# Two narrow self-attentions on one core: scores on 32-row tiles, the mask as a bf16 product, key blocks on GpSimd, Newton steps for the roots

## The chip, the core and the metric

The kernel runs on one core of a Trainium2 chip. The metric is the device time of the whole program in microseconds. A profiled execution gives the span from the first to the last instruction and everything that happened in it.

## The reference, cut to what matters

The program is a decoder layer stack of six phases on 128 sequences of 64 tokens with 128 features: a wide self-attention, a narrow cross-attention, a feed-forward block, two narrow self-attentions (one global, one local), a wide cross-attention and a last product with tanh. Only the two narrow self-attentions change.

```
def rmsnorm(x, w): return x * rsqrt(mean(x * x) + 1e-6) * w
def qk_norm(x):    return x * rsqrt(mean(x * x) + 1e-6)
q = split_heads(x @ wq, 16)          # 16 heads of 8 features
k, v = split_heads(..., 4)           # 4 key/value heads, each for 4 query heads
q, k = qk_norm(rope(q)), qk_norm(rope(k))
scores = where(mask, q @ k.T / sqrt(8), -1e30)   # causal; local: also i - j < 32
out = merge_heads(softmax(scores) @ v) @ wo
...
h = layernorm(x)
h = h + global_attention(rmsnorm(h)); h = h + local_attention(rmsnorm(h)); x = x + h
```

## The kernel before

Activations stay in SBUF: X (`w_x`) and the working copy H (`w_h`), both as 64 tiles of 128 tokens (two sequences) by 128 features. Each phase is a block in which every engine runs its own program, and `narrow_self_attention(k, local)` makes the global stage (tiles named `gl_`) and the local one (`lo_`). In each program `skewed(engine, 64, [(lag, piece), ...], unroll)` writes out the order by hand: in step u the engine runs each piece, in the list's order, on tile u minus its lag. `after(engine, semaphore, t, back)` makes the engine wait until tile t-back has passed a point. An engine's queue is in order, so a waiting piece holds back everything behind it in its list.

The path of a tile, with lines of the kernel before:
- VectorE normalises it. In the global stage it takes statistics of X, GpSimd takes the root (`rsqrt`, L1832), VectorE writes H (L1699), then takes the root mean square of H by a second set of statistics (L1707 to L1726), GpSimd takes that root (`rms_rsqrt`, L1838), VectorE writes `hn` (L1732). The local stage has the second half alone.
- TensorE turns `hn` (`turn`, L1571), ScalarE copies it out (L1634), TensorE projects to queries, keys and values (L1579, 192 columns).
- VectorE rotates queries and keys (L1739 to L1749), squares them (L1756) and sums each head (L1762, 20 columns); GpSimd raises the 20 sums to the power -0.5 (`qk_rsqrt`, L1844); VectorE multiplies (`qk_apply`, L1775 and L1776).
- TensorE transposes the queries in four pieces of 32 columns and the keys in one (L1587, L1588). ScalarE copies the queries (L1650, 32x512) and writes the keys four times, scaled by a 0/1 column per key head, so that the other heads' rows are zero (`key_blocks`, L1658).
- `scores` (L1597) is four fp32 products of 128 weight columns by 256 query columns, run as eight passes. Rows 64 to 127 of both operands hold an identity and the mask, written once at the start (L1805 to L1814), so that the same product adds the mask. Each half goes to its own PSUM bank and ScalarE takes the exponential of each (L1666).
- ScalarE spreads the values out (L1642, four short copies), TensorE multiplies probabilities and values (`attend`, L1609, 32 passes), VectorE divides (L1782, L1789), TensorE turns it (L1617), ScalarE copies (L1672), TensorE applies the output weights (L1622), and VectorE adds the residual (L1795 or L1797).

Other phases have instructions of the same kinds: the narrow cross-attention scores on 32-row tiles and makes its key blocks on GpSimd (L1245), the wide one scores on 64-row tiles (L845) and scales its probabilities on GpSimd (L1016). Every normalisation there adds epsilon and takes a root on GpSimd (L486, L489), and VectorE applies it (L496).

## Time and profile before

| what | us |
|---|---|
| median of 3 runs (2473.71 to 2476.63) | 2474.64 |
| the profiled execution, its own time | 2471.66 |
| its span | 2469.6 |
| TensorE busy over the span | 2181.6 (88%) |
| VectorE busy | 1927.5 (78%) |
| ScalarE busy | 1490.9 (60%) |
| GpSimd busy | 1224.1 (50%) |

In the rows, PE is TensorE's products and PEld its weight loads, DVE is VectorE, ACT is ScalarE, POOL is GpSimd. "128*64" is the part of the array in use, "<-" reads "written from". Idle time before a group is followed by what ended most of it. The global stage lies at about 1081 to 1400 us of the span, the local one at 1401 to 1705.

### The profile page before, as it was taken

To read this page: it belongs to the slowest core of one execution; us is meant where nothing else is said; L and a number is where in the kernel's file an instruction comes from. 1 tells how busy PE (TensorE), PEld (TensorE's weight loads), DVE (VectorE), ACT (ScalarE), POOL (GpSimd) and SP (SyncE) were. 2 spreads that over 40 slices of the span, in tenths; PEclk is the share of its full clock that TensorE was granted. 3 is DMA by queue.
4 is the path that set the end of the run, shared out by engine and by line. 5 is a ranking of instruction groups with operands and counts; after the bars stand their busy time and mean duration, and the time that the engine had idled before them with its cause. 6 is when DMAs were issued, how large, how long until landed. Compare 5 with 4: busy or idle time off the path is not lost. (4 is left out here: it accounts for less than half of the span.)

```text
span 2469.6 us, 90130 instructions
## 1 busy us (share of the span) xinstructions
PE 2181.6 (88%) x33103; PEld 1800.1 (73%) x33103; DVE 1927.5 (78%) x5481; ACT 1490.9 (60%) x3973; POOL 1224.1 (50%) x1215
## 2 busy tenths in 40 slices
PE   7999999977777753439999799998999999999998
PEld 7888888865555541228888588886888888888886
...
DMA packets 56943, 25.66 MB, mean 10 GB/s; under 512 B 18115, under 2 KB 56326, under 8 KB 56838
## 3 DMA queue, kind: packets, MB, share of 16 engines
...
q14 instruction: 38, 0.31, 0.0%
...
## 5 line engine op out<-in xcount | busy, mean ns | idle before, releaser
L706 POOL TENSOR_TENSOR sa_sc<-sa_sc,sa_rs 128x1024 f32<-128x1024 f32 x64 | 121.9, 1904 | 314.3 <-DVE sa_rs L682 314.3
L1844 POOL TENSOR_TENSOR lo_qk_r<-lo_qk_ms,w_neg_half 128x20 f32<-128x20 f32 x64 | 226.8, 3544 | 21.9 <-DVE lo_qk_ms L1767 21.9
L1844 POOL TENSOR_TENSOR gl_qk_r<-gl_qk_ms,w_neg_half 128x20 f32<-128x20 f32 x64 | 227.0, 3546 | 1.4 <-DVE gl_qk_ms L1767 1.3
L486 POOL TENSOR_TENSOR xan_ve<-xan_mv,w_eps_ln 128x1 f32<-128x1 f32 x64 | 12.1, 189 | 400.5 <-DVE xan_mv L480 400.5
L892 ACT ACTIVATE xa_cT<-xa_misc 128x128 f32<-128x128 f32 x64 | 17.8, 277 | 304.9 <-PE xa_misc L793 273.6
L1016 POOL TENSOR_TENSOR xa_sc<-xa_sc,xa_rs 128x1024 f32<-128x1024 f32 x64 | 121.7, 1902 | 119.1 <-DVE xa_rs L976 119.1
L821 PEld LDWEIGHTS xa_qs<-xan_xT,late_x_wq 128*128 128x128 f32 x1024 | 120.0, 193 | 52.8 <-issue 52.8
L973 DVE TENSOR_REDUCE xa_sm<-xa_sc 128x16 f32<-128x1024 f32 x64 | 78.1, 1220 | 71.6 <-ACT xa_sc L916 71.6
L1236 POOL TENSOR_TENSOR ca_sc<-ca_sc,ca_mx 128x1024 f32<-128x1024 f32 x64 | 121.8, 1902 | 24.1 <-DVE ca_mx L1206 24.1
L558 PE MATMUL sa_qs<-san_xT,w_a_wq 128*128 128x128 f32 x1024 | 130.3, 281 | 2.7 <-DVE sa_sc L668 2.2
L821 PE MATMUL xa_qs<-xan_xT,late_x_wq 128*128 128x128 f32 x1024 | 132.2, 283 | 0.0
L832 PE MATMUL xa_pp<-xa_cT,late_x_wk 128*128 128x128 f32 x1024 | 131.1, 281 | 0.0
L1597 PE MATMUL lo_ss<-lo_qT,lo_kz 128*128 128x256 f32 x512 | 127.9, 393 | 1.3 <-ACT lo_kz L1658 0.9
L878 PE MATMUL xa_yy<-late_x_wo,xa_oT 128*128 128x128 f32 x1024 | 126.6, 277 | 2.5 <-ACT xa_oT L930 2.5
L1597 PE MATMUL gl_ss<-gl_qT,gl_kz 128*128 128x256 f32 x512 | 127.4, 392 | 1.3 <-ACT gl_kz L1658 0.9
L930 ACT ACTIVATE xa_oT<-xa_oo 128x512 f32<-128x512 f32 x128 | 69.4, 594 | 97.6 <-PE xa_oo L868 97.6
L810 PE MATMUL xa_oo<-late_x_wv,xa_cT 128*64 128x512 f32 x512 | 125.7, 612 | 0.7 <-ACT xa_cT L892 0.7
L603 PE MATMUL sa_yy<-w_a_wo,sa_oT 128*128 128x128 f32 x1024 | 124.9, 275 | 1.2 <-ACT sa_oT L651 1.2
L679 DVE TENSOR_REDUCE sa_sm<-sa_sc 128x16 f32<-128x1024 f32 x64 | 78.1, 1220 | 59.2 <-ACT sa_sc L637 59.2
L558 PEld LDWEIGHTS sa_qs<-san_xT,w_a_wq 128*128 128x128 f32 x1024 | 120.7, 194 | 4.8 <-DVE sa_sc L668 4.8
L878 PEld LDWEIGHTS xa_yy<-late_x_wo,xa_oT 128*128 128x128 f32 x1024 | 121.1, 194 | 2.7 <-ACT xa_oT L930 2.7
L832 PEld LDWEIGHTS xa_pp<-xa_cT,late_x_wk 128*128 128x128 f32 x1024 | 119.1, 191 | 4.2
...
## 6 DMA issues: line engine op xcount, KB each, us to landing
...
```

Source lines behind the costliest of these rows:

```text
L558: last = pe.matmul(qs[b][:, c * P:(c + 1) * P], k["a_wq"][:, ch * P:(ch + 1) * P], norm["xT"][:, s, :], start=True, stop=True)
L603: last = pe.matmul(yy[:, 0:D], oT[:, s, n % 2, n // 2, :], k["a_wo"][:, n, :], start=(n == 0), stop=(n == 7))
L679: dve.tensor_reduce(sm[:, s, :], sc[:, s, :, :, :].rearrange("p e c j -> p (e c) j"), AX.X, ALU.add).then_inc(sum_done, 1)
L706: pool.tensor_tensor(v, v, bcast(rs[:, s, :], 2, S), ALU.mult).then_inc(prob_done, 1)
L810: final = pe.matmul(oo[order][r * 64:r * 64 + 64, :].rearrange("p (m c) -> p m c", m=4), cT[:, s, b * 64:b * 64 + 64], wv[:, :, r, :], sta ...
L821: final = pe.matmul(qs[b][:, c * P:(c + 1) * P], k["x_wq"][:, ch * P:(ch + 1) * P], norm["xT"][:, s, :], start=True, stop=True)
L832: final = pe.matmul(pp[b][:, c * P:(c + 1) * P], k["x_wk"][:, ch * P:(ch + 1) * P], cT[:, s, :], start=True, stop=True)
L878: final = pe.matmul(yy[:, 0:D], oT[:, s, n % 2, n // 2, :], k["x_wo"][:, n, :], start=(n == 0), stop=(n == 7))
L1016: pool.tensor_tensor(v, v, bcast(rs[:, s, :], 2, S), ALU.mult).then_inc(prob_done, 1)
L1236: pool.tensor_tensor(sc[:, four, :, :], sc[:, four, :, :], bcast(mx[:, s, :], 2, S), ALU.subtract).then_inc(shifted, 1)
L1597: last = pe.matmul(ss[b][:, g * 256:(g + 1) * 256], kz[:, s, b, 2 * g:2 * g + 2, :].rearrange("p g j -> p (g j)"), qT[:, s, b, :, :].rearr ...
L1844: pool.tensor_tensor(qk_r[:, s, :], qk_ms[:, s, :], k["neg_half"][:, 0:NQK], ALU.pow).then_inc(sg["qk_r"], 1)
```

## The change

- The mask is no longer part of the scores' operands. Four bf16 products of an identity with the mask (`identb`, `maskb`) start the four PSUM banks, one for each query head of a group; 16 fp32 products on 32-row tiles, one tile for each such head, add the scores. One semaphore step reports all of them.
- Queries and keys are transposed by two products of 128 columns; the keys are written four times side by side by VectorE (`kn`). ScalarE copies both in one instruction. GpSimd writes the key blocks in one multiplication of 128x512.
- The 20 roots for each tile are no longer a power. VectorE halves the sums and makes a first guess by integer arithmetic on their bits, for two tiles at once; GpSimd refines it by three Newton steps of four instructions on 40 columns, each waiting for the one before.
- In the global stage the second set of statistics goes: both roots come from the first variance, in one power of two columns, and `hn` is written from X.
- One PSUM bank (`tr`) holds the first transpose and the two of queries and keys, with waits that keep their writes and reads apart. Lags and orders change; TensorE and ScalarE are unrolled by eight, with eight value buffers.

```diff
+SEED = float(0x5f3759df - 0x400000)
...
+        identb, maskb = sb("identb", [P, P], BF16), sb("maskb", [P, 4, S], BF16)
...
-                    pe.transpose(misc[:, 0:P], hn[:, s, :], ident).then_inc(sg["hT_psum"], 1)
+                    after(pe, sg["qT"], t, 6)
+                    pe.transpose(tr[:, 0:P], hn[:, s, :], ident).then_inc(sg["hT_psum"], 1)
...
                     after(pe, sg["qkn"], t, per=2)
                     after(pe, sg["qT"], t, 1)
-                    after(pe, sg["k_blocks"], t, 1, per=KVG)
+                    pe.wait_ge(sg["hT"], min(t + 5, NT) if isinstance(t, int) else t + 5)
+                    pe.transpose(tr[:, P:2 * P], qn[:, s, :, :, :].rearrange("p r g d -> p (r g d)"), ident)
+                    pe.transpose(tr[:, 2 * P:3 * P], kn[:, s, :, :, :].rearrange("p r g d -> p (r g d)"), ident).then_inc(sg["qkT_psum"], 1)
+                def scores(t, four):
+                    s = four % 2
+                    after(pe, sg["exp"], t, 1, per=2)
                     for r in range(4):
-                        pe.transpose(tq[0:32, r * P:(r + 1) * P], qn[:, s, r, :, :].rearrange("p g d -> p (g d)"), ident)
-                    pe.transpose(tk[0:32, 0:P], kn[:, s, :, :].rearrange("p g d -> p (g d)"), ident).then_inc(sg["qkT_psum"], 1)
-                def scores(t, four):
-                    s = four % 2
+                        pe.matmul(ss[:, r, 0:256], identb[:, :], maskb[:, :, :].rearrange("p n i -> p (n i)"), start=True, stop=False)
                     after(pe, sg["qT"], t)
-                    after(pe, sg["k_blocks"], t, per=KVG)
+                    after(pe, sg["k_blocks"], t)
+                    gate(k, pe)
                     for b in range(2):
-                        after(pe, sg["exp"], t, 1, per=2)
                         for g in range(2):
-                            last = pe.matmul(ss[b][:, g * 256:(g + 1) * 256],
-                                             kz[:, s, b, 2 * g:2 * g + 2, :].rearrange("p g j -> p (g j)"),
-                                             qT[:, s, b, :, :].rearrange("p r i -> p (r i)"), start=True, stop=True)
-                        last.then_inc(sg["scores_psum"], 1)
...
+                                                 kz[q, s, b, 2 * g:2 * g + 2, :].rearrange("p g j -> p (g j)"),
+                                                 qkT[q, s, 0, b * 64:b * 64 + 64], start=False, stop=(b == 1 and g == 1))
+                    last.then_inc(sg["scores_psum"], 1)
...
-                skewed(pe, NT, [(4, turn_queries_keys), (6, turn_out), (2, project), (5, attend), (6, output), (1, turn), (4, scores)], 4)
+                skewed(pe, NT, [(6, turn_queries_keys), (1, turn), (2, project), (7, attend), (8, turn_out), (6, scores), (8, output)], 8)
...
-                def queriesT(t, four):
+                def queries_keysT(t, four):
...
-                    after(act, sg["scores_psum"], t, 2, per=2)
-                    act.activation(qT[0:32, s, :, :, :].rearrange("p b r i -> p r b i"),
-                                   tq[0:32, :].rearrange("p (r b i) -> p r b i", r=4, b=2), ACT.Copy).then_inc(sg["qT"], 1)
...
-                    after(act, sg["scores_psum"], t, 2, per=2)
-                    for g in range(KVG):
-                        act.activation(kz[0:32, s, :, g, :], tk[0:32, 0:P].rearrange("p (b j) -> p b j", b=2), ACT.Copy,
-                                       scale=groups[0:32, g:g + 1]).then_inc(sg["k_blocks"], 1)
+                    act.wait_ge(sg["hT_psum"], min(t + 6, NT) if isinstance(t, int) else t + 6)
+                    after(act, sg["scores_psum"], t, 2)
+                    after(act, sg["k_blocks"], t, 2)
+                    act.activation(qkT[:, s, :, :].rearrange("p n i -> p (n i)"), tr[:, P:3 * P], ACT.Copy).then_inc(sg["qT"], 1)
...
-                    for b in range(2):
-                        act.wait_ge(sg["scores_psum"], t * 2 + b + 1)
-                        act.activation(pr[:, s, :, b, :], ss[b][:, :].rearrange("p (n i) -> p n i", i=S), ACT.Exp,
+                    after(act, sg["scores_psum"], t)
+                    for r in (0, 2):
+                        act.activation(pr[:, s, r:r + 2, :, :, :].rearrange("p r b g i -> p r (b g i)"), ss[:, r:r + 2, 0:256], ACT.Exp,
...
-                skewed(act, NT, [(4, queriesT), (6, outT), (4, key_blocks), (2, values), (1, turned), (4, exponent)], 4)
+                skewed(act, NT, [(6, queries_keysT), (1, turned), (8, outT), (2, values), (6, exponent)], 8)
...
+                    dve.tensor_scalar(ve[:, s, 0:1], mv[:, s, 1:2], EPS_LN, None, ALU.add).then_inc(sg["var_eps"], 1)
+                    dve.tensor_scalar(ve[:, s, 1:2], mv[:, s, 1:2], 1.0 + EPS_RMS, EPS_LN * EPS_RMS, ALU.mult,
...
-                    dve.tensor_scalar(tile_of(H, t), tile_of(X, t), mv[:, s, 0:1], rstd[:, s:s + 1],
+                    after(dve, sg["hT_psum"], t, 2)
+                    dve.tensor_scalar(hn[:, s, :], tile_of(X, t), mv[:, s, 0:1], rstd[:, s, 1:2],
+                                      ALU.subtract, ALU.mult).then_inc(sg["normed"], 1)
...
+                def hidden_itself(t, four):
+                    s = four % 2
+                    dve.tensor_scalar(tile_of(H, t), tile_of(X, t), mv[:, s, 0:1], rstd[:, s, 0:1],
                                       ALU.subtract, ALU.mult).then_inc(sg["hidden"], 1)
...
-                    after(dve, sg["squared"], t, 2)
...
+                    after(dve, sg["qkn"], t, 4, per=2)
+                    dve.tensor_tensor(rot[:, four, :, :], rc[:, s, :, :], rsn[:, s, :, :], ALU.add).then_inc(sg["rotated"], 1)
...
-                def qk_epsilon(t, four):
...
-                    dve.tensor_scalar(qk_ms[:, s, :], qk_ms[:, s, :], HD * EPS_RMS, None, ALU.add).then_inc(sg["qk_mse"], 1)
+                    dve.tensor_reduce(qk_ms[:, four, :], sq[:, s, :, :], AX.X, ALU.add).then_inc(sg["qk_ms"], 1)
...
+                def qk_halve(t, four):
+                    if four % 2:
...
+                        dve.tensor_scalar(qk_half[:, p, :], qk_ms[:, p, :], HD * EPS_RMS, 0.5, ALU.add, ALU.mult).then_inc(sg["qk_half"], 2)
+                def qk_seed(t, four):
...
+                        dve.tensor_scalar(qk_r[:, p, :].bitcast(I32), qk_half[:, p, :].bitcast(I32), -0.5, SEED, ALU.mult,
+                                          ALU.add).then_inc(sg["qk_seed"], 2)
...
-                    dve.tensor_tensor(kn[:, s, :, :], rot[:, s, HEADS:NQK, :], bcast(qk_r[:, s, HEADS:NQK], 2, HD), ALU.mult).then_inc(sg["qkn"], 1)
+                    dve.tensor_tensor(kn[:, s, :, :, :], bcast(rot[:, four, HEADS:NQK, :], 1, 4),
+                                      bcast(bcast(qk_r[:, four, HEADS:NQK], 2, HD), 1, 4), ALU.mult).then_inc(sg["qkn"], 1)
...
-                dve.memset(qT[:, :, :, :, :], 0.0).then_inc(sg["zeroed"], 1)
-                dve.memset(kz[:, :, :, :, :], 0.0).then_inc(sg["zeroed"], 1)
-                dve.wait_ge(sg["zeroed"], 3)
-                for n in range(2):
-                    for b in range(2):
-                        dve.tensor_copy(qT[64:P, n, b, :, :], bcast(ident[64:P, 64:P], 1, 4)).then_inc(sg["masked"], 1)
-                        dve.tensor_copy(kz[64:P, n, b, :, :], bcast(mask[64:P, :], 1, KVG)).then_inc(sg["masked"], 1)
+                dve.tensor_copy(identb[:, :], ident).then_inc(sg["masked"], 1)
+                dve.tensor_copy(maskb[:, :, :], bcast(mask, 1, 4)).then_inc(sg["masked"], 1)
...
-                    skewed(dve, NT, [(4, qk_apply), (7, residual), (0, rms_measure), (1, rms_apply), (7, residual_x), (0, rms_mean),
+                    skewed(dve, NT, [(6, qk_apply), (1, rms_apply), (9, residual), (0, rms_measure), (9, residual_x), (0, rms_mean),
                                      (2, rotate), (0, rms_square), (2, rotate_sum), (0, rms_epsilon), (2, qk_measure),
-                                     (5, invert_sums), (2, qk_sum), (5, divide), (2, qk_epsilon)], 4)
+                                     (7, invert_sums), (2, qk_sum), (7, divide), (2, qk_halve), (2, qk_seed)], 4)
                 else:
-                    skewed(dve, NT, [(6, qk_apply), (9, residual), (0, hidden), (1, normed_hidden), (3, rms_apply), (0, hidden_mean),
-                                     (2, rms_measure), (0, hidden_epsilon), (2, rms_mean), (4, rotate), (2, rms_square),
-                                     (4, rotate_sum), (2, rms_epsilon), (4, qk_measure), (7, invert_sums), (4, qk_sum),
-                                     (7, divide), (4, qk_epsilon)], 4)
+                    skewed(dve, NT, [(6, qk_apply), (1, normed_hidden), (9, residual), (0, hidden), (1, hidden_itself),
+                                     (0, hidden_mean), (2, rotate), (0, hidden_epsilon), (2, rotate_sum), (2, qk_measure),
+                                     (7, invert_sums), (2, qk_sum), (7, divide), (2, qk_halve), (2, qk_seed)], 4)
...
+                    after(pool, sg["rms_var_eps"], t)
                     after(pool, sg["hidden"], t, 2)
-                    pool.tensor_tensor(rstd[:, s:s + 1], ve[:, s:s + 1], k["neg_half"][:, 0:1], ALU.pow).then_inc(sg["rstd"], 1)
+                    after(pool, sg["normed"], t, 2)
+                    pool.tensor_tensor(rstd[:, s, :], ve[:, s, :], k["neg_half"][:, 0:2], ALU.pow).then_inc(sg["rstd"], 1)
...
-                    pool.tensor_tensor(qk_r[:, s, :], qk_ms[:, s, :], k["neg_half"][:, 0:NQK], ALU.pow).then_inc(sg["qk_r"], 1)
-                shift = 0 if local else 2
-                front = [] if local else [(0, rsqrt)]
-                skewed(pool, NT, front + [(shift, rms_rsqrt), (2 + shift, qk_rsqrt)], 4)
+                    if four % 2 == 0:
+                        return
+                    p = slice(four - 1, four + 1)
+                    y, y2 = qk_r[:, p, :], qk_a[:, p, :]
+                    for n in range(3):
+                        if n == 0:
+                            after(pool, sg["qk_seed"], t)
+                        else:
+                            pool.wait_ge(sg["qk_step"], t - 1 + n)
+                        done = (t - 1) * 3 + 2 * n + 2
+                        pool.tensor_tensor(y2, y, y, ALU.mult).then_inc(sg["qk_y2"], 2)
+                        pool.wait_ge(sg["qk_y2"], done)
+                        pool.tensor_tensor(y2, y2, qk_half[:, p, :], ALU.mult).then_inc(sg["qk_hy2"], 2)
+                        pool.wait_ge(sg["qk_hy2"], done)
+                        pool.tensor_tensor(y2, three_halves[:, :, :], y2, ALU.subtract).then_inc(sg["qk_rest"], 2)
+                        pool.wait_ge(sg["qk_rest"], done)
+                        last = pool.tensor_tensor(y, y, y2, ALU.mult)
+                        if n < 2:
+                            last.then_inc(sg["qk_step"], 1)
+                        else:
+                            last.then_inc(sg["qk_r"], 2)
+                def key_blocks(t, four):
+                    s = four % 2
+                    after(pool, sg["qT"], t)
+                    after(pool, sg["scores_psum"], t, 2)
+                    pool.tensor_tensor(kz[:, s, :, :, :].rearrange("p b g j -> p g b j"),
+                                       bcast(qkT[:, s, 1, :].rearrange("p (b j) -> p b j", b=2), 1, KVG),
+                                       bcast(bcast(groups, 2, 2), 3, S), ALU.mult).then_inc(sg["k_blocks"], 1)
+                pool.memset(three_halves[:, :, :], 1.5).then_inc(sg["constant"], 1)
+                pool.wait_ge(sg["constant"], 1)
+                skewed(pool, NT, [(6, key_blocks), (0, rms_rsqrt if local else rsqrt), (2, qk_rsqrt)], 4)
```

## Rows read from the trace of the kernel before

**Rows 1.** Busy us by window: PE, PEld, DVE, ACT, POOL, then granted clock; global, local
```profile
...
1200.00:1360.00 160.00, 158.80 (x1793) 129.36 (x1791) 134.37 (x739) 133.97 (x458) 160.00 (x107) 1.00 0.00 0
...
1500.00:1650.00 150.00, 150.00 (x1738) 126.24 (x1737) 108.37 (x615) 128.60 (x445) 138.16 (x70) 1.00 0.00 0
...
```

**Rows 2.** Timeline of GpSimd, global stage, one tile: start us, length us, instruction
```profile
...
1247.26 3.53 POOL L1844 TENSOR_TENSOR gl_qk_r<-gl_qk_ms,w_neg_half 128x20 f32<-128x20 f32 x1
1250.77 0.54 POOL L1832 TENSOR_TENSOR gl_rstd<-gl_ve,w_neg_half 128x1 f32<-128x1 f32 x1
1251.28 0.62 POOL L1838 TENSOR_TENSOR gl_rms<-gl_ms,w_neg_half 128x1 f32<-128x1 f32 x1
1251.80 3.53 POOL L1844 TENSOR_TENSOR gl_qk_r<-gl_qk_ms,w_neg_half 128x20 f32<-128x20 f32 x1
...
```

**Rows 3.** Timeline of TensorE, local stage, one tile: start, length, instruction, count
```profile
...
1553.04 1.96 PE L1597 MATMUL lo_ss<-lo_qT,lo_kz 128*128 128x256 f32 x8
1554.84 0.60 PE L1587 MATMUL lo_tq<-w_constant,lo_qn 128*32 128x128 f32 x4
...
1555.39 0.27 PE L1617 MATMUL lo_yy<-w_constant,lo_o 128*128 128x128 f32 x1
1555.50 0.49 PE L1579 MATMUL lo_qkv<-w_s_w,lo_hT 128*128 128x192 f32 x2
1555.92 1.11 PE L1609 MATMUL lo_av<-lo_vz,lo_pr 128*64 128x18 f32 x32
1556.96 0.49 PE L1622 MATMUL lo_yy<-w_s_wo,lo_oT 128*128 128x128 f32 x2
1557.29 0.27 PE L1571 MATMUL lo_misc<-w_constant,lo_hn 128*128 128x128 f32 x1
1557.43 1.97 PE L1597 MATMUL lo_ss<-lo_qT,lo_kz 128*128 128x256 f32 x8
```

**Rows 4.** Groups of ScalarE, local stage, 1500 to 1650: busy us, mean ns | idle
```profile
...
L1666 ACT ACTIVATE lo_pr<-lo_ss 128x512 f32<-128x512 f32 x68 | 40.6, 597 | 17.8 <-PE lo_ss L1597 17.8
...
L1642 ACT ACTIVATE lo_vz<-lo_qkv 64x16 f32<-64x16 f32 x138 | 24.0, 174 | 2.5
...
```

**Rows 5.** Line L1597, scores: min/median/max ns, first and last start in us
```profile
...
L1597 PE MATMUL gl_ss<-gl_qT,gl_kz x512: 379/379/767, 1107.8 to 1395.7; 128*128 128x256 f32 x171
...
L1597 PE MATMUL lo_ss<-lo_qT,lo_kz x512: 379/379/767, 1418.9 to 1699.9; 128*128 128x256 f32 x171
...
```

**Rows 6.** Timeline of VectorE at the start of the local stage
```profile
...
1401.24 0.30 DVE L1805 MEMSET lo_vz<- 128x288 f32 x1 [0.94 <-PEq L164]
...
1405.77 0.29 DVE L1707 BATCH_NORM_STATS2 lo_rstats<-w_h 128x6 f32<-128x128 f32 x1
```

**Rows 7.** Timeline of TensorE, wide cross-attention: scores on 64-row tiles, next instruction
```profile
...
2004.30 1.16 PE L845 MATMUL xa_qs<-xa_kT,xa_qT 64*64 64x64 f32 x64
2005.44 0.30 PE L779 MATMUL xa_misc<-w_constant,xan_xn 128*128 128x128 f32 x1
...
```

**Rows 8.** Line L1154, ScalarE's copy of 128x256 from PSUM
```profile
...
L1154 ACT ACTIVATE ca_xcT<-ca_m x64: 382/383/402, 549.2 to 885.1; 128x256 f32<-128x256 f32 x64
...
```

**Rows 9.** Line L1245, GpSimd's key blocks of the narrow cross-attention
```profile
...
L1245 POOL TENSOR_TENSOR ca_kz<-ca_kT,w_constant x64: 1041/1042/1045, 551.8 to 890.1; 128x512 f32<-128x512 f32 x64
...
```

**Rows 10.** Timeline of GpSimd, wide cross-attention: one instruction, one that needs it
```profile
...
1904.93 0.19 POOL L486 TENSOR_TENSOR xan_ve<-xan_mv,w_eps_ln 128x1 f32<-128x1 f32 x1 [6.13 <-DVE xan_mv L480]
1905.20 0.55 POOL L489 TENSOR_TENSOR xan_rstd<-xan_ve,w_neg_half 128x1 f32<-128x1 f32 x1
...
```

**Rows 11.** Line L1016, GpSimd's product of 128x1024
```profile
...
L1016 POOL TENSOR_TENSOR xa_sc<-xa_sc,xa_rs x64: 1899/1902/1905, 1725.0 to 2448.8; 128x1024 f32<-128x1024 f32 x64
...
```

**Rows 12.** Timeline of GpSimd, narrow cross-attention: the same two instructions
```profile
...
730.44 0.19 POOL L486 TENSOR_TENSOR can_ve<-can_mv,w_eps_ln 128x1 f32<-128x1 f32 x1 [0.99 <-DVE can_mv L480]
730.78 0.55 POOL L489 TENSOR_TENSOR can_rstd<-can_ve,w_neg_half 128x1 f32<-128x1 f32 x1 [0.16 <-POOL can_ve L486]
...
```

**Rows 13.** Line L496, VectorE's normalisation in the wide cross-attention
```profile
...
L496 DVE TENSOR_SCALAR xan_xn<-w_x,xan_mv,xan_rstd x64: 340/997/1009, 1707.3 to 2428.2; 128x128 f32 x48, 128x128 f32<-128x128 f32 x16
...
```

85 lines of the change are left out of this document (43 added, 42 removed).

## The prediction

> **What bounds the kernel now.** I read the busy time by window first. The two self-attention stages are steady, at the full 2.4 GHz clock. In the global stage GpSimd is busy for all of 160 us and TensorE for 158.8; in the local stage TensorE for all of 150 us, GpSimd for 138 and ScalarE for 129 [rows 1]. So there are two near-equal bounds, and the reader has to look inside a tile to see which sets the period. In the global stage GpSimd runs one 3.53 us power on 20 columns and two of about 0.54 us on one column, back to back, and starts the next tile's 4.54 us after the last [rows 2]: GpSimd is the bound. In the local stage TensorE has no gap in a tile of 4.39 us [rows 3]: scores 1.80 (1553.04 to 1554.84), five transposes of queries and keys 0.55, transpose of the output 0.11, projection 0.42, values product 1.04, output 0.33, first transpose 0.14. ScalarE's exponentials take 0.597 us each, two a tile [rows 4]. From first to last score, 63 intervals, the stages take 287.9 and 281.0 us [rows 5]. The profiled execution took 2471.66 us around a span of 2469.6; the median of the runs is 2474.64, 3.0 more. I work the sum on the profiled one and add 3.0.
>
> **The change, part by part.** *TensorE's own work.* Three of five transposes go (3 x 0.11); two remain, of 128 columns, taken as 0.12 each: 0.24 for 0.55 [rows 3]. The eight score passes of 256 columns, 0.225 each [rows 3], give way to four bf16 mask products of 256 columns and 16 products on 32-row tiles, which as fp32 are 32 passes. No row has a bf16 product here: at most one fp32 pass each (0.90 for four), at least a quarter of the time of both passes of a product (0.45). I take 0.45, since these need one pass of 256 columns where the fp32 form needs two slower ones. For the 32 passes the nearest row is the wide cross-attention's 64 passes on four 64x64 tiles, 1.14 us with the change-over at both ends, 0.94 without [rows 7]: 0.059 a pass on its own tile. There too a tile has 64 moving columns, but 64 weight columns; here it has 128. If the weights set the pace a pass takes twice as long: eight to a tile, 8 x 0.118 = 0.94; if the moving columns do, 0.47. I take 0.94, and 0.1 for each change of tile shape (half of 1.14 less 0.94). TensorE's sum falls from 4.39 to 4.39 - 0.31 - 1.80 + 0.45 + 0.94 + 0.20 = 3.87.
>
> The Trainium skill, "TensorE: Matmul & The Clock Gate", section LDWEIGHTS, says a load's time follows its columns, not its rows, so cutting products to 32 rows would save nothing on loads. By that, with the tiles loading in turn, the 32 passes would cost 32 x 0.107 = 3.4 us, an estimate from that page. The 64 passes in [rows 7] fit tiles that load beside each other; that case is priced as a rival.
>
> *ScalarE.* The four scaled copies of the keys go and the 512-column copy becomes one of 256 columns, 0.38 [rows 8]. The values' four short copies and the exponentials stay [rows 4]. Its sum falls well under the period; only the order of its work matters below.
>
> *GpSimd.* Key blocks: 128x512 with two broadcasts, the same instruction shape as the narrow cross-attention's, 1.04 us a tile [rows 9]. Newton: 12 dependent products of 40 columns for each pair of tiles, each waiting for the one before by a semaphore. A one-column instruction lasts 0.19 and the next, dependent one starts 0.27 after it [rows 10]; per column the long form costs (1.902 - 1.042) / 512 = 1.7 ns [rows 9, 11], so 40 columns add 0.06: 0.33 each, 12 x 0.33 = 3.96 a pair. Below, 0.27 if the columns are free (3.24); above, 0.34 [rows 12] plus 0.06 plus rounding, 0.41 (4.92). The global stage's power on two columns costs 0.54 + 0.16 (a column is (3.53 - 0.54) / 19) = 0.70, the local one's 0.54 [rows 2]. A pair of global tiles is 2 x (1.04 + 0.70) + 3.96 = 7.44, or 3.7 a tile where it was 4.54. By sums alone everything gets faster.
>
> *VectorE.* The global stage loses the second set of statistics, the local one nothing much; the additions in small columns go to pairs, the keys' product grows from 32 to 128 columns (about 0.1). It was busy 134 of 160 us [rows 1] and falls; its cover is the period itself, and I cost it at nothing as long as a tile lasts over 4 us. The two memsets of 0.91 and eight copies ahead of the stage give way to two copies: 4.5 us of setup [rows 6] becomes about 1.7, a gain of 2.8. No DMA is added or moved.
>
> **The order of the work is what I think decides.** Keys now pass through four engines, and GpSimd's queue is in order: key blocks of tile u-6, the root of tile u, and on odd steps the whole Newton chain. Two loops follow, with handoffs of 0.05 to 0.1.
> Loop A, key blocks to the next key blocks: blocks 1.04, to TensorE 0.10, scores' products to their last result 0.94 + 0.22, to ScalarE 0.05, two exponentials 1.15, then, behind them in ScalarE's queue, the next queries-and-keys copy 0.33, to GpSimd 0.08: 3.91.
> Loop B, scores to scores: 1.16 + 0.05 + 1.15, to TensorE 0.07, values product 1.04 (it stands ahead of the scores in TensorE's queue and waits for the exponentials), output transpose 0.11, masks 0.45, change-over 0.10: 4.13. So TensorE's 3.87 is not reached; 4.13 would be.
> On an odd step GpSimd does blocks 1.04, root 0.70, chain 3.96 and 0.08 of handoff, 5.78, before it can take the next blocks, although these are ready after 3.9. TensorE waits for them with the scores, and behind them stand output, the next transposes, projection and values: nothing can run ahead, so the late time isn't made up on the even step, when GpSimd idles. A pair takes 5.78 + 3.91 = 9.69 us in the global stage and 9.53 in the local one (root 0.54), 4.84 and 4.77 a tile against 4.54 and 4.39. Key blocks of tile t run in step t+6 and chains in the odd steps 3 to 65, so the intervals after tiles 1, 3 ... 59 carry a chain, 30 of the 63: global 30 x 9.69 + 3 x 4.13 = 303.1, +15.2; local 30 x 9.53 + 12.4 = 298.3, +17.3 [rows 5]. Front edge: locally scores begin two steps later; four steps took 1405.77 to 1418.9, 3.3 each [rows 5, 6], so 6.6 less 2.8 of setup, +3.8; globally the depth stays at six and I put +1 for the chains. Sum +37.3: 2509.0 for the profiled execution, 2512 as a median. The new waits of the shared transpose bank (queries-and-keys copy behind the next first transpose) ask only for a 0.11 us transpose that directly follows; nothing.
>
> **Rivals.**
> 1. *Forecast, the chain blocks the key blocks* (chance 0.52): 2512, from 2469 (3.24 a chain: 60 chains x 0.72 = 43 less) to 2570 (4.92: 58 more).
> 2. *The burst is absorbed* (0.27), the other side: the place is GpSimd's queue between two key blocks. If the chain is short enough, or the loop through ScalarE long enough, that 5.78 fits, a pair takes 2 x 4.13 = 8.26. Global 63 x 4.13 = 260.2, -27.7; local -20.8; with edges +4.8, -43.7: 2431. For it: all sums fall, and one-off spans on GpSimd are rough. Against: [rows 10] have even a one-column instruction at 0.27. It decides from where a pair falls 37.3 / 60 = 0.62 under my 9.6, to about 9.0: a chain of some 3.3 us.
> 3. *The chain waits for VectorE* (0.12). A normalisation from SBUF to SBUF took 0.997 us beside GpSimd's long product and 0.340 otherwise [rows 13]: the two engines do hold each other up. If each chain product meets such a VectorE instruction 40% of the time (some six a tile, near 0.3 us like the one in [rows 6], in 4.8) and waits half of it, that is 0.06 x 12 = 0.7 a pair, +43: 2555. Against: the 3.53 us powers keep their length with VectorE's additions beside them [rows 2].
> The Trainium skill, "SBUF — State Buffer", section "Who interferes with whom", has this rule: VectorE instructions with two SBUF inputs, or in a two-port mode, lock GpSimd out. The trace bears out the second half only, and only in the other direction.
> 4. *Row tiles load in turn* (0.04): 32 passes of 0.118 are 3.8 us, 2.8 more. In a pair the chain hides this on one tile; on the other it lengthens loop A: 60 x 2.8 = 168, about 2680. [Rows 7] speak against it.
> 5. *It nets out* (0.05): shorter handoffs and a chain near 3.3.
>
> **Numbers.** Predicted 2512. The range 2440 to 2572 holds the forecast's own 2469 to 2570, rival 3 and the upper part of rival 2. Measurements tell 0.2%, 5 us, from no change. Faster 0.29 (rival 2, a little of 1), within 0.07, slower 0.64.
>
> **What the next profile would show.** Right: GpSimd's chain of 12 in a row, then key blocks at once; TensorE's scores waiting for key blocks on every second tile for 1.5 us or so, tile spacings alternating near 4 and 5.7; TensorE's busy share in both stages at some 80%. Wrong: even spacings near 4.1; chain products starting under 0.28 apart; scores' products far from 1 us; the values product waiting where I have the scores wait.

## The result: 2809 us where 2475 stood and 2512 was forecast

The changed kernel takes 2809.0 us in the median (2808.1 to 2809.3, three runs) against 2474.64: a ratio of 1.1355, 95% interval [1.1338, 1.1373]. The sign was forecast, the size was not: the result lies 237 us above the top of the range. The profiled execution has a span of 2807.2 us, 337.6 more than before.

The page of the changed kernel's profile, engine totals and three lines of the 40 slices:

```profile
PE 2503.7 (89%) x36303; PEld 2068.2 (74%) x36303; DVE 1991.5 (71%) x5273; ACT 1329.2 (47%) x3461; POOL 1099.3 (39%) x1921
...
PE   7999999877777243999999699999989999999998
...
POOL 0333333377776301444444344444312222222222
PEclk8999999999999675555555555555589999999999
```

Read the last line first. Over both narrow stages, slices 16 to 29 of the 40, the granted clock of TensorE is 5 tenths, 1.2 GHz, where it was 9 or more before outside the stage borders. TensorE's digits beside it are 9, but for the stage borders. Both kernels enter the global stage at 0.5; this is the kernel before, just ahead of its first scores (busy time of PE, PEld, DVE, ACT, POOL, then the clock):

```profile
1094.00:1108.00 14.00, 5.54 (x16) 3.15 (x17) 11.59 (x64) 4.17 (x19) 10.63 (x10) 0.50 0.00 0
```

It came to 1.0 at about 1114 us and kept it to the stage's end. The changed kernel never came to it. One stretch in each of its stages, the answer to [rows 1]:

```profile
1250.00:1400.00 150.00, 150.00 (x1627) 124.56 (x1627) 89.08 (x389) 54.09 (x193) 73.38 (x175) 0.50 0.00 0
1700.00:1850.00 150.00, 150.00 (x1633) 124.37 (x1630) 87.66 (x385) 53.71 (x194) 70.97 (x175) 0.50 0.00 0
```

TensorE is busy in every microsecond, GpSimd for half of them. The line of the scores' products, the answer to [rows 5], says what this costs:

```profile
L1606 PE MATMUL gl_ss<-gl_qkT,gl_kz x2048: 416/416/472, 1122.6 to 1561.8; 32*128 32x64 f32 x187
...
L1606 PE MATMUL lo_ss<-lo_qkT,lo_kz x2048: 416/416/472, 1597.5 to 2036.6; 32*128 32x64 f32 x187
```

First to last score: 439.2 and 439.1 us where there were 287.9 and 281.0, that is +151.3 and +158.1. The first score comes 14.8 later, the gap between the stages is 12.5 longer, and behind the last score 0.9 is added: together 337.6, the whole difference. The per-tile work is in the timeline of TensorE, one global tile, the answer to [rows 3]:

```profile
1300.52 1.90 PE L1618 MATMUL gl_av<-gl_vz,gl_pr 128*64 128x18 f32 x32
1302.35 0.48 PE L1626 MATMUL gl_yy<-w_constant,gl_o 128*128 128x128 f32 x1
1302.62 1.06 PE L1598 MATMUL gl_ss<-gl_maskb,gl_identb 128*128 128x256 bf16 x4
1303.61 1.99 PE L1606 MATMUL gl_ss<-gl_qkT,gl_kz 32*128 32x64 f32 x32
1305.53 0.80 PE L1631 MATMUL gl_yy<-w_s_wo,gl_oT 128*128 128x128 f32 x2
1306.12 0.42 PE L1591 MATMUL gl_tr<-w_constant,gl_qn 128*128 128x128 f32 x1
1306.33 0.42 PE L1592 MATMUL gl_tr<-w_constant,gl_kn 128*128 128x128 f32 x1
1306.54 0.42 PE L1576 MATMUL gl_tr<-w_constant,gl_hn 128*128 128x128 f32 x1
1306.76 0.85 PE L1584 MATMUL gl_qkv<-w_s_w,gl_hT 128*128 128x192 f32 x2
1307.53 1.90 PE L1618 MATMUL gl_av<-gl_vz,gl_pr 128*64 128x18 f32 x32
```

Take start to start: values 1.83, masks 0.99, scores 1.92, and so on to 7.0 us a tile (1300.52 to 1307.53), with no gap. The forecast's sum has 1.04, 0.45 and 1.04 for these three, at 2.4 GHz: each takes about twice as long. GpSimd's timeline (the chain's first products, then the key blocks behind its last one) has the structure of the forecast in it all the same:

```profile
1310.62 0.25 POOL L1862 TENSOR_TENSOR gl_qk_a<-gl_qk_r 128x40 f32<-128x40 f32 x1 [1.17 <-DVE gl_qk_r L1779]
1311.02 0.27 POOL L1864 TENSOR_TENSOR gl_qk_a<-gl_qk_a,gl_qk_half 128x40 f32<-128x40 f32 x1
1311.43 0.27 POOL L1866 TENSOR_TENSOR gl_qk_a<-gl_three_halves,gl_qk_a 128x40 f32<-128x40 f32 x1
...
1314.97 0.27 POOL L1868 TENSOR_TENSOR gl_qk_r<-gl_qk_r,gl_qk_a 128x40 f32<-128x40 f32 x1
1315.20 1.04 POOL L1878 TENSOR_TENSOR gl_kz<-gl_qkT,w_constant 128x512 f32<-128x512 f32 x1
```

The products last 0.25 to 0.27 but start 0.35 to 0.41 apart: a chain is 4.6 us from 1310.62 to the key blocks at 1315.20. At 1.2 GHz TensorE's 14 us a pair hide it.

### The profile page after: what moved, and what is told of

The parts are those of the page before. It is cut to its first block and busy times, and to the rows that moved or that the text cites. A ratio compares the mean times of both kernels' runs of the same rounds, so it can differ in the third digit from the quotient of the medians.

```text
span 2807.2 us, 96939 instructions
## 1 busy us (share of the span) xinstructions
PE 2503.7 (89%) x36303; PEld 2068.2 (74%) x36303; DVE 1991.5 (71%) x5273; ACT 1329.2 (47%) x3461; POOL 1099.3 (39%) x1921
## 5 line engine op out<-in xcount | busy, mean ns | idle before, releaser
L1606 PEld LDWEIGHTS lo_ss<-lo_qkT,lo_kz 32*128 32x128 f32 x2048 | 115.2, 323 | 29.4 <-issue 29.4
L1606 PEld LDWEIGHTS gl_ss<-gl_qkT,gl_kz 32*128 32x128 f32 x2048 | 115.1, 323 | 29.4 <-issue 29.4
L1618 PEld LDWEIGHTS lo_av<-lo_vz,lo_pr 128*64 128x64 f32 x2048 | 114.5, 224 | 28.7 <-issue 25.0
L1618 PEld LDWEIGHTS gl_av<-gl_vz,gl_pr 128*64 128x64 f32 x2048 | 114.5, 224 | 28.7 <-issue 25.0
L1237 POOL TENSOR_TENSOR ca_sc<-ca_sc,ca_mx 128x1024 f32<-128x1024 f32 x64 | 121.8, 1903 | 23.9 <-DVE ca_mx L1207 23.8
L1667 ACT ACTIVATE lo_pr<-lo_ss 128x512 f32<-128x512 f32 x128 | 69.5, 595 | 129.0 <-PE lo_ss L1606 129.0
L1606 PE MATMUL lo_ss<-lo_qkT,lo_kz 32*128 32x64 f32 x2048 | 127.2, 423 | 3.2 <-issue 3.2
L1606 PE MATMUL gl_ss<-gl_qkT,gl_kz 32*128 32x64 f32 x2048 | 127.2, 423 | 3.2 <-issue 3.2
L1667 ACT ACTIVATE gl_pr<-gl_ss 128x512 f32<-128x512 f32 x128 | 69.5, 595 | 127.4 <-PE gl_ss L1606 127.4
L1878 POOL TENSOR_TENSOR gl_kz<-gl_qkT,w_constant 128x512 f32<-128x512 f32 x64 | 68.4, 1069 | 147.2 <-ACT gl_qkT L1660 145.1
```

What stands on the lines that cost most here:

```text
L1237: pool.tensor_tensor(sc[:, four, :, :], sc[:, four, :, :], bcast(mx[:, s, :], 2, S), ALU.subtract).then_inc(shifted, 1)
L1606: last = pe.matmul(ss[:, r, (2 * b + g) * 64:(2 * b + g) * 64 + 64], kz[q, s, b, 2 * g:2 * g + 2, :].rearrange("p g j -> p (g j)"), qkT[q, ...
L1618: last = pe.matmul(av[b * 64:b * 64 + 64, n * 2 * VW:(n + 1) * 2 * VW], pr[:, s, n % 4, b, n // 4, :], vz[:, eight, n // 4, b, :, :].rearr ...
L1667: act.activation(pr[:, s, r:r + 2, :, :, :].rearrange("p r b g i -> p r (b g i)"), ss[:, r:r + 2, 0:256], ACT.Exp, scale=HD * float(HD) ** ...
```

## Experiments

Two questions: what keeps the clock down, and what the change is worth where the clock is full. The times are of one execution each, but for the last kernel; the kernel before took 2465 to 2477 us beside them. Where the text gives a time per tile for a whole stage, it is first to last score over the 63 intervals. Some recorded expectations have 5.53, 5.33, 4.54 and 7.26 us instead. These were taken between ScalarE's first and last copies of `hT`, which take in the quick first steps and leave out the last ones; the scores of the same runs give 5.67, 5.55, 4.64 and 7.61. "Parted" stands for a Newton chain parted over two steps.

### Does the level keep itself, or does the stream of products lose it?

The changed kernel with one burst of dense products in each stage:

```diff
+                    if isinstance(t, int) and t == 9:
+                        for n in range(24):
+                            pe.matmul(ss[:, n % 4, 256:512], ident, k["constant"][:, 0:256], start=True, stop=True)
```

> The changed kernel, with 24 dense fp32 products of 256 columns into unused PSUM columns, once in each stage, at step 15 ahead of the masks (extra work, results unused). The changed kernel had a granted clock of 0.50 from 1024 us to 2052 us, all of both stages. Theory C (the stream is too light: the new mix of products never earns the 2.4 GHz level, whatever came before): the clock may rise during the burst and falls back, tile spacing stays near 7.0 us, total 2805 to 2840 us. Theory H (either level keeps itself: the stream would hold 2.4 GHz if it once had it): clock 1.0 behind the burst to the end of the stage, about 50 tiles of each stage at 4.8 to 5.3 us, total 2560 to 2620 us.

Measured: 2825.05 us, inside the range of theory C. By window, before the burst, behind it, and later (columns as above):

```profile
1150.00:1189.00 39.00, 39.00 (x390) 32.34 (x389) 20.21 (x95) 13.29 (x49) 18.27 (x44) 0.50 0.01 2
1190.00:1213.00 23.00, 20.47 (x268) 16.86 (x266) 11.28 (x52) 7.30 (x27) 7.56 (x18) 1.00 0.01 2
1220.00:1400.00 180.00, 180.00 (x1944) 149.39 (x1942) 106.07 (x461) 65.22 (x234) 86.96 (x206) 0.50 0.00 0
```

The clock came, stayed 23.9 us in each stage, and went. Behind the burst stand the products of the changed kernel, and in the first stage the level fell at 1213.9, at the end of TensorE's first long pause behind a chain (the 2.73 us below). These 24 us also show the change itself at 2.4 GHz, TensorE first, then GpSimd:

```profile
1197.57 0.60 PE L1601 MATMUL gl_ss<-gl_maskb,gl_identb 128*128 128x256 bf16 x4
1198.10 1.12 PE L1609 MATMUL gl_ss<-gl_qkT,gl_kz 32*128 32x64 f32 x32
...
1202.40 1.12 PE L1609 MATMUL gl_ss<-gl_qkT,gl_kz 32*128 32x64 f32 x32
...
1213.97 1.98 PE L1609 MATMUL gl_ss<-gl_qkT,gl_kz 32*128 32x64 f32 x32 [2.73 <-issue]
```
```profile
1205.16 1.04 POOL L1881 TENSOR_TENSOR gl_kz<-gl_qkT,w_constant 128x512 f32<-128x512 f32 x1 [2.52 <-ACT gl_qkT L1663]
...
1212.83 1.04 POOL L1881 TENSOR_TENSOR gl_kz<-gl_qkT,w_constant 128x512 f32<-128x512 f32 x1
```

Masks 0.53 for four, scores 4.30 apart without a chain, key blocks 7.67 apart with one; TensorE idles 2.73 us before the scores behind the chain. The scores before that pause start 4.31 apart (1202.40 to 1206.71), those across it 7.26.

Two dense float32 products a tile, whose result nobody reads, ahead of the masks:

```diff
...
+                    for n in range(2):
+                        pe.matmul(ss[:, n, 256:512], ident, k["constant"][:, 0:256], start=True, stop=True)
```

> The changed kernel with two dense fp32 products of 256 columns more in every tile (extra work, results unused). If the clock stays at 0.50 they cost 1.8 us a tile: 128 x 1.8 = 230 more, about 3040 us. Theory C: the added dense work earns the clock back, granted clock 1.0 in both stages, and although there is more work the time falls, to about 2500 to 2570 us (tile 4.6 to 5.3 us, set by GpSimd's chain ahead of the key blocks as I forecast). A theory that TensorE is slow for another reason (row tiles, code fetch) gives 3040.

The changed kernel with identity and mask as float32 (eight dense passes for four):

```diff
-        identb, maskb = sb("identb", [P, P], BF16), sb("maskb", [P, 4, S], BF16)
+        identb, maskb = sb("identb", [P, P]), sb("maskb", [P, 4, S])
```

> The changed kernel with identity and mask in fp32 instead of bf16, one part undone. At half clock the four products take twice 0.99 us: 128 x 0.99 = 127 more, about 2935 us, if the clock stays down. Theory C: eight dense passes instead of four may earn the clock back; then about 2500 to 2570 us. If it was the bf16 type itself that cost the clock, this alone brings it back.

Measured: 2662.45 and 2651.11 us. More work on TensorE, and 147 and 158 us less time; both lie over theory C's 2500 to 2570, by 92 and 81. The window 1200 to 1350, first of the fill, then of the float32 mask:

```profile
1200.00:1350.00 150.00, 129.46 (x2122) 106.51 (x2121) 104.33 (x483) 64.26 (x242) 90.37 (x216) 1.00 0.00 0
```
```profile
1200.00:1350.00 150.00, 139.72 (x2122) 116.04 (x2121) 109.20 (x475) 63.52 (x239) 90.09 (x213) 1.00 0.00 0
```

TensorE is busy for a smaller share than in the changed kernel and has the full clock. (With the fill the level was not quite steady: over the two stages it averaged 0.95 and 0.94, with the float32 mask 1.00 and 0.98.) GpSimd in the float32 mask's run:

```profile
1302.55 1.09 POOL L1878 TENSOR_TENSOR gl_kz<-gl_qkT,w_constant 128x512 f32<-128x512 f32 x1
...
1306.41 1.04 POOL L1878 TENSOR_TENSOR gl_kz<-gl_qkT,w_constant 128x512 f32<-128x512 f32 x1 [2.08 <-ACT gl_qkT L1660]
...
1309.06 0.25 POOL L1862 TENSOR_TENSOR gl_qk_a<-gl_qk_r 128x40 f32<-128x40 f32 x1 [0.87 <-DVE gl_qk_r L1779]
...
1313.84 1.10 POOL L1878 TENSOR_TENSOR gl_kz<-gl_qkT,w_constant 128x512 f32<-128x512 f32 x1
```

Key blocks 3.86 apart without a chain (forecast: 3.91), 7.43 with one (5.78), of which 0.87 is a wait for VectorE's seed and 4.78 the chain. So at full clock too the chain decides, and harder than forecast: 5.67 us a tile in this stage.

### Is it the amount of work or its kind?

Each bfloat16 mask product twice in a row, and, in a kernel of its own, each set of score products twice:

```diff
+                        pe.matmul(ss[:, r, 0:256], identb[:, :], maskb[...], start=True, stop=True)
```
```diff
+                    for twice in range(2):
...
```

> The changed kernel with each of its four bfloat16 mask products issued twice in a row, the second added onto the first, so that the mask counts double in the scores (the output is therefore that of a doubled mask). It asks whether TensorE's clock came back in the run with the mask in float32 because the products are of another type, or because they keep TensorE at work longer. The bfloat16 products took 0.99 us for four at 1.2 GHz. If the amount of work is what matters (theory C in its plain form), the granted clock returns to 2.4 GHz over most of the stages and the time falls to 2620 to 2720 us. If four more bfloat16 products bring nothing, the clock stays at 0.5 and 128 tiles pay 0.9 to 1.0 us each: 2809 + 115 to 127 = 2925 to 2940 us.

(In the edit both products of a bank start it anew, so the second replaces the first and the mask counts once. The work on TensorE is the doubled one all the same.)

> The changed kernel with its 32 score products on 32 rows issued twice over, the second set added onto the first (so the scores count double against the mask and the output is that of doubled scores). Each set took 1.92 us at 1.2 GHz and 1.05 at 2.4. It asks whether more float32 work of the narrow kind brings the clock back, as four wide float32 mask products do. If any float32 work counts alike, the 32 more products (1.05 us at full clock, against 1.4 for the float32 masks) bring 2.4 GHz over most of the stages and the time lies between 2640 and 2760 us. If products that read 32 rows and few columns weigh as little as the first set seems to, the clock stays at 0.5 and 128 tiles pay 1.9 us each: 2809 + 245 = 3040 to 3070 us.

Measured: 2916.96 and 3053.74 us, the second reading of each (the doubled masks 8 us under its lower end). The doubled masks in 1200 to 1350:

```profile
1200.00:1350.00 150.00, 150.00 (x1531) 122.67 (x1532) 73.51 (x343) 47.85 (x171) 63.48 (x150) 0.50 0.00 1
```

Neither brought the clock back at all. The doubled masks are as many passes, of the same rows and columns, as the four float32 products that lift it; the doubled scores are float32, but narrow, and add 1.71 us a tile at 1.2 GHz (8.72 for 7.01 in most steps). So in these runs added busy time alone did not lift the clock; the kind of product matters.

### What the chain costs at full clock

The float32 mask again, six of the chain's twelve products in step t + 2 and six in t + 3 (the semaphores between them stay):

```diff
-                skewed(pool, NT, [(6, key_blocks), (0, rms_rsqrt if local else rsqrt), (2, qk_rsqrt)], 4)
+                skewed(pool, NT, [(6, key_blocks), (0, rms_rsqrt if local else rsqrt),
+                                  (2, lambda t, four: newton(t, four, 0)), (3, lambda t, four: newton(t, four, 1))], 4)
```

> The changed kernel with the mask in float32 (granted clock 1.0 in most of both stages, 2651.1 us) and GpSimd's twelve Newton operations of a pair parted over two steps: six behind the values of step t + 2 and six a step later. It asks whether the chain, standing whole ahead of one tile's key blocks, is what still holds that kernel at 5.53 us a tile. The forecast's own theory: a pair costs one loop of 3.9 and one of 7.2 now, and with six operations (6 x 0.41 = 2.46) in each step, step for step about 1.04 + 2.46 + values behind the wait fit beside the other engines' 4.4 to 4.9; so 4.6 to 5.0 us a tile, in all 2651 - 128 x 0.55 to 0.9 = 2535 to 2580 us. The rival: the order in which the engines pass a tile round, or VectorE, holds the kernel, and the chain only fills GpSimd's idle time; then the time stays within 15 us of 2651.

Measured: 2612.68 us, 38 less, 27.7 of it between the stages' first and last scores (now 5.55 and 5.50 us a tile); that is half the least gain of the first reading, and more than the rival allows. Most of what holds it now is TensorE's own sum with float32 masks, busy for 142.1 of 150 us (1250 to 1400): 1.82 for the masks, start to start, in place of 0.53 adds 1.29 to a tile of about 3.94 (1198.10 to 1202.40 above, less a wait of 0.36), which makes 5.23.

### One or two of the four mask products in float32

Parted chain, with one and with two of the four mask products in float32:

```diff
+                        if r < 1:
+                            pe.matmul(ss[:, r, 0:256], ident, mask32[:, :, :].rearrange("p n i -> p (n i)"), start=True, stop=False)
+                        else:
                             pe.matmul(ss[:, r, 0:256], identb[:, :], maskb[...], start=True, stop=False)
```

> The changed kernel with the Newton chain parted over two steps, as in the run that took 2612.7 us and 5.33 us a tile with all four mask products in float32; here only one of the four is in float32 and three are in bfloat16. A float32 mask product took 0.47 us there (1.89 for four at 2.4 GHz), a bfloat16 one should take about 0.12 at 2.4 GHz (0.25 at 1.2 GHz). If one dense float32 product a tile keeps the 2.4 GHz level, TensorE's sum is 5.33 - 3 x 0.35 = 4.28 us; with GpSimd's 5.8 to 6.3 a pair and the loops between, 4.3 to 4.7 us a tile, in all 2612.7 - 128 x 0.63 to 1.03 = 2480 to 2532 us. If it is too little, the stages run at 1.2 GHz, where TensorE's 7.01 us a tile grow by one product at the half clock: 2800 to 2900 us. Anything between means that the level changes to and fro.

> As the one before, with two of the four mask products in float32 and two in bfloat16. Two float32 products added to the changed kernel brought 2.4 GHz back over most of the stages. Where the level holds: 5.33 - 2 x 0.35 = 4.63 us a tile, 4.6 to 4.9 with the loops, 2525 to 2560 us. If the level changes to and fro, 2600 us or more.

Measured: two, 2542.98 us, inside the first reading, clock 1.0 in both stages but for the global stage's first 16 us. One, 2695.33 us, between its two readings, and this is the strangest profile of the study; one window of each stage:

```profile
1200.00:1350.00 150.00, 145.26 (x2478) 114.62 (x2481) 136.35 (x580) 78.78 (x293) 110.30 (x259) 1.00 0.00 0
1600.00:1750.00 150.00, 150.00 (x1514) 122.05 (x1514) 74.06 (x351) 49.47 (x175) 64.52 (x158) 0.50 0.00 0
```

The same code and the same products: the first stage keeps 2.4 GHz from its first scores to its end (4.64 us a tile), the second 1.2 GHz to its end (7.61). So the kernel ran again with the burst in the second stage alone:

```diff
+                    if local and isinstance(t, int) and t == 9:
+                        for n in range(24):
...
```

> The run with one float32 mask product a tile took 2695.3 us: its first stage ran wholly at the granted clock of 1.0 from 1118 us on, at 4.54 us a tile, its second wholly at 0.5, at 7.26 us a tile, though both issue the same products. Here 24 dense float32 products of 256 columns stand once, at step 15 of the second stage alone (about 9 us), in columns that nobody reads. After such a burst the changed kernel, with no float32 product of that kind, held 2.4 GHz for 23.9 us and fell back. Theory now: with one dense product a tile the stream lies at the edge and the level keeps itself (at 1.0 the same products follow each other faster); then the second stage stays at 1.0 after the burst, some 48 tiles save 2.7 us each, and the time is 2695 + 9 - 130 = 2560 to 2600 us. The rival: the second stage's stream is too light whatever the level before it, and the clock falls back within some 30 us: 2695 to 2710 us.

Measured: 2553.17 us, 7 under the first reading's lower end. The second stage before and after the burst:

```profile
1440.00:1490.00 50.00, 49.91 (x504) 40.05 (x504) 25.51 (x119) 17.09 (x61) 23.26 (x58) 0.50 0.01 2
1510.00:1660.00 150.00, 141.95 (x2323) 113.88 (x2324) 123.26 (x526) 72.09 (x265) 96.12 (x233) 1.00 0.00 1
```

The 24 products that nobody reads took 12.4 us, the first of them at 1.2 GHz, and brought 142 back. The first stage, which has no burst here, rose by itself again. The first burst run's answer ("the level does not keep itself") was right for that stream only: this one holds either level, whichever it is put on.

### Is it the pause behind the chain?

The changed kernel with its bfloat16 masks and the parted chain (the edit of the run that parts the chain, above, alone), and the same with the first burst's edit too:

> The changed kernel with nothing else altered than GpSimd's Newton chain, parted over two steps (all four mask products stay in bfloat16). At 1.2 GHz TensorE's sum of 7.01 us a tile hides the chain in either form, so if the clock stays at 0.5 the time stays at 2795 to 2815 us. If it is the pause behind the whole chain that keeps the clock down, the granted clock comes to 1.0 in both stages, at 4.3 to 4.6 us a tile: 2470 to 2520 us.

> As the run before, with 24 dense float32 products once in each stage at step 15, as in the burst runs. If the pause behind the whole chain is what let the clock fall back after 23.9 us there, it now stays at 1.0 from about 1190 us on in the first stage and in the second: some 48 tiles of each stage at 4.3 to 4.5 us instead of 7, 2809 + 18 - 96 x 2.6 = 2560 to 2600 us. If a stream with no dense float32 mask product is too light whatever its pauses, the clock falls back within some 30 us in each stage: 2800 to 2830 us. A level that holds for some 100 us and then falls would say that it is near the edge.

Measured: 2800.8 us, at 1.2 GHz throughout both stages, inside the first range, and 2666.12 us, between its two. With the burst:

```profile
1200.00:1300.00 100.00, 95.39 (x1641) 73.42 (x1640) 91.48 (x390) 53.83 (x196) 74.97 (x175) 1.00 0.00 1
1320.00:1370.00 50.00, 48.26 (x837) 37.15 (x835) 46.11 (x198) 27.16 (x99) 37.96 (x89) 1.00 0.00 0
...
1700.00:1850.00 150.00, 150.00 (x1619) 124.46 (x1617) 80.96 (x383) 54.54 (x193) 70.23 (x171) 0.50 0.00 0
```

By the trace's record of the granted clock it held 242 us in the first stage, to 1420, some seven us behind the last projection and ahead of the last four tiles' scores, and 68 in the second, against 23.9 twice with the whole chain. This is the third outcome named. The pause behind the whole chain therefore goes with a shorter time at full clock, but without it the stream is still not one that rises to 2.4 GHz by itself, and it may fall from it.

It also gives the price of the changed order at full clock with the worst of the chain gone: 4.60 us a tile (43 tiles, 1203.3 to 1396.3), no better than the 4.54 of before in that stage [rows 2]. TensorE is at 95 of 100 us and VectorE at 91.5, and TensorE's largest wait for another engine there is for VectorE's keys (groups of TensorE, 1200 to 1400; after the bar, idle time and releaser):

```profile
L1591 PE MATMUL gl_tr<-w_constant,gl_qn 128*128 128x128 f32 x44 | 14.4, 328 | 8.4 <-DVE gl_kn L1792 8.2
```

### The other parts alone

The Newton steps put into the kernel before, with that kernel's own order of steps, scores and key blocks (two lines of the edit):

```diff
...
-                                     (7, divide), (4, qk_epsilon)], 4)
+                                     (7, divide), (4, qk_halve), (4, qk_seed)], 4)
```

> The kernel before with the Newton steps on tile pairs alone; scores, key blocks on ScalarE and normalisations as before. Theory C: TensorE's stream is the one of before, so the clock stays at 1.0. GpSimd's 4.54 us a tile in the global stage fall to about 3.6, TensorE's 4.39 is left: 64 x 0.15 = 10 less, local stage within 5 us: 2455 to 2475 us. If the Newton burst is what costs the clock, this run shows 0.5 in both stages and over 2700 us.

Measured: 2986.43 us, a clear miss. Waits of 1150 to 1350 us (waited for: total, times, longest):

```profile
DVE gl_qn L1787 <- POOL gl_qk_r L1869: 53.4, 11, 4.9
...
PE gl_tq L1592 <- DVE gl_kn L1788: 47.7, 11, 4.4
```

In that order VectorE wants the roots of a pair at once after it has made the seed, so every pair stalls all engines for a chain, 4.9 us. TensorE was busy 151 of 200 us and its clock averaged 0.70: the record has 6.8 us at 1.0 and 10.2 at 0.5 in turn, once for each pair. I had taken the chain's length without looking at the steps between seed and use. So next, with the steps that the change has (scores and keys at 6, values product at 7, output at 8) and its fused normalisation (TensorE's line of the edit):

```diff
...
-                skewed(pe, NT, [(4, turn_queries_keys), (6, turn_out), (2, project), (5, attend), (6, output), (1, turn), (4, scores)], 4)
+                skewed(pe, NT, [(6, turn_queries_keys), (8, turn_out), (2, project), (7, attend), (8, output), (1, turn), (6, scores)], 8)
```

> The kernel before with its own scores, masks and key blocks, and from the change only the Newton steps on tile pairs, the fused normalisation in both stages, and the later steps for scores, attention and output that the change gives them. So the products that TensorE runs are those of before. It asks whether the new scores alone took TensorE's clock down, and whether the Newton steps are harmless once a whole step lies between seed and use. Theory C: the granted clock is 1.0 over both stages (after the same dip at a stage's start) and the tiles pass at 4.35 to 4.45 us in both stages: 2455 to 2480 us. If the Newton steps hold the loop all the same, as they did with the old steps (2986 us), the tiles pass at 5 us or more and the time is over 2550 us, whatever the clock.

And the fused normalisation alone, with the old power for queries and keys (its first lines):

```diff
...
-                    dve.tensor_scalar(ve[:, s:s + 1], mv[:, s, 1:2], EPS_LN, None, ALU.add).then_inc(sg["var_eps"], 1)
+                    dve.tensor_scalar(ve[:, s, 0:1], mv[:, s, 1:2], EPS_LN, None, ALU.add).then_inc(sg["var_eps"], 1)
+                    dve.tensor_scalar(ve[:, s, 1:2], mv[:, s, 1:2], 1.0 + EPS_RMS, EPS_LN * EPS_RMS, ALU.mult,
+                                      ALU.add).then_inc(sg["rms_var_eps"], 1)
...
```

> The kernel before with one thing from the change: the first stage takes both of its normalisations from one set of moments, with one root of two columns on GpSimd, and passes its tiles at the local stage's steps. Scores, mask, roots of queries and keys stay. The first stage now passes a tile in 4.54 us and the second, which has that normalisation already in part, in 4.39. If VectorE's shorter chain is what parts the two, 64 tiles gain up to 0.15 us each and the time falls by up to 10 us, to 2464 to 2470 us (ratio 0.996 to 0.998). If TensorE's sum alone sets both, the time stays within 2 us of the kernel before.

Measured: 2481.28 us, and 2463.33 (nine runs), ratio to the 2472.14 of before beside it 0.9965 [0.9954, 0.9976]; the first 1 us over its range, the second 1 under. The scores' lines of the two:

```profile
L1602 PE MATMUL gl_ss<-gl_qT,gl_kz x512: 378/379/767, 1117.3 to 1399.5; 128*128 128x256 f32 x171
...
L1602 PE MATMUL lo_ss<-lo_qT,lo_kz x512: 378/379/763, 1430.6 to 1713.1; 128*128 128x256 f32 x171
```
```profile
L1597 PE MATMUL gl_ss<-gl_qT,gl_kz x512: 379/379/766, 1108.7 to 1390.2; 128*128 128x256 f32 x171
...
L1597 PE MATMUL lo_ss<-lo_qT,lo_kz x512: 379/379/766, 1413.5 to 1694.7; 128*128 128x256 f32 x171
```

Inside the stages both take 281 to 283 us, at a granted clock of 1.00 (windows 1150 to 1350 and 1450 to 1650 of the first). With room for it the Newton chain costs at most some 1.3 us a stage there, and gains nothing. The 18 us between the two are mostly edges: with the chain and the later steps the first scores come 8.6 later and the stages' gap is 7.8 longer. The fused normalisation frees GpSimd in the global stage, whose 63 intervals go from 287.9 us [rows 5] to 281.5, to what the local stage takes (281.2). It is the only part that gained in a run of its own, and with it alone the kernel is faster than both, though by 0.35% only. The new scores were never run at full clock in the old order, so what they are worth there by themselves is not shown.

## Why the forecast was wrong

**The failed step: "The two stages are steady, at the full 2.4 GHz clock."** This was read from [rows 1] and then kept as a constant of the sum, while the sum took from TensorE the very products that went with it: eight dense float32 passes of 256 columns. Nothing in the section on costs or the rivals asked whether the clock would stay. With TensorE at 1.2 GHz its 3.87 us became 7.0, above every loop, and 63 intervals took 439 us where 303.1 and 298.3 were forecast: 277 of the 300 us missed on the profiled execution (337.6 less 37.3). The rest is edges: 14.8 + 12.5 + 0.9 = 28.2, against 4.8. That miss is not the clock's: ahead of the first scores the kernel before stood at 0.5 too, and the run with the old scores, the chain and the later steps, at full clock inside its stages, has 9.5 and 7.9 of the 14.8 and 12.5. The forecast had +1 and +3.8 for these two. Of the signs that I had named, the chain of twelve with the key blocks at once behind it was there; TensorE waiting for them, its share of 80% and the spacings of 4 and 5.7 were not: it was at 100%, and a tile took 7.0. That the scores' form is the cause is shown from both sides: float32 masks bring the clock back within the changed kernel, and the old scores, with the transposes and key blocks that go with them, keep it beside the Newton steps, the fused normalisation and the later steps.

The Trainium skill, "TensorE: Matmul & The Clock Gate", Part 1, says that the gate's level follows how busy TensorE has been. The rows agree only if "busy" is not the busy time that the profile lists: 150.00 of 150.00 us went with 0.50, and 129.46 of 150.00 with 1.00.

**TensorE's terms** were right at full clock: masks 0.53 for 0.45, scores to the next product 1.05 (1198.10 to 1199.15) for 0.94 and 0.1 of change-over, loop B 4.30 for 4.13. The 0.45 was a choice between two bounds, without a row of its kind; it came out near. Rival 4, row tiles that load in turn, falls: that would have been 3.8 us.

**GpSimd, a second step that failed.** Key blocks 1.04 as taken in most rows, loop A 3.86 for 3.91. The chain was mis-sized: 4.78 us, 0.40 a product, for 3.96 and 0.33, near the upper bound of 4.92. And a term was missing: behind the root GpSimd waits 0.87 for VectorE's seed. So 7.43 and 7.67 stand for 5.78. A pair took 7.43 + 3.86 = 11.3 with float32 masks and 4.31 + 7.26 = 11.6 in the burst's 24 us, where 9.69 was forecast. So the forecast would have missed at full clock too: 60 pairs at 1.7 more each make about 100 us, some 2610, above the range. This is an estimate from these pairs; no run held the full clock for a whole stage with the whole chain and bfloat16 masks. Forecast mechanism 1 is shown by the chain ahead of the key blocks and by the gain of parting it (38 us), but it isn't what set the time of the changed kernel: parting the chain there left 2800.8 for 2809.0, 8 us, all of it at the stages' edges (439.1 us from first to last score in both stages still).

**VectorE** was costed at nothing "as long as a tile lasts over 4 us". At 1.2 GHz that held. At 2.4 GHz it didn't: 91.5 of 100 us with the parted chain, 84% before [rows 1]. Its instructions with two inputs in SBUF stretch beside the key blocks, here the squares:

```profile
1301.73 1.05 DVE L1760 TENSOR_TENSOR gl_sq<-gl_rot 128x160 f32<-128x160 f32 x1
```

This is the changed kernel; the key blocks ran from 1301.38 to 1302.60 (1.22 for 1.04), and the same form took 0.32 beside a root in the run with parted chain and float32 masks. Rival 3 had the right pair of engines but not the main cost: the chain's products start 0.35 to 0.41 apart in the rows above. In the burst's 24 us at full clock three of the twelve start 0.51 to 0.56 apart, as this one, beside VectorE's sum `gl_rot<-gl_rc,gl_rsn` of 1210.28:

```profile
1210.30 0.43 POOL L1869 TENSOR_TENSOR gl_qk_a<-gl_three_halves,gl_qk_a 128x40 f32<-128x40 f32 x1
1210.81 0.28 POOL L1871 TENSOR_TENSOR gl_qk_r<-gl_qk_r,gl_qk_a 128x40 f32<-128x40 f32 x1
```

That chain took 5.02 us (1207.81 to 1212.83) for 4.58 in the changed kernel: 0.4, where rival 3 had 0.7. The Trainium skill, "SBUF — State Buffer", section "Who interferes with whom", has the lock between a VectorE instruction with two SBUF inputs and a GpSimd instruction that reads SBUF; here that agrees.

**Rival 2**, the burst absorbed and 2431 us, was wrong both ways: no kernel with the change's scores came near 2431, not even where the parted chain ran at full clock, at 4.60 us a tile.

What stays open: which property of a product counts for the clock. For the wide masks the type alone parts the runs, but a float32 pass also lasts longer (1.82 us for eight, against 0.53 for four in bfloat16); for the float32 scores rows and columns were not told apart. The stream with one float32 mask was seen in two executions, and without a burst both rose in the first stage and stayed down in the second; why is not shown, and two executions don't exclude chance. The whole chain with a full clock and bfloat16 masks was seen for 24 us at a time only.
